# Edge loop of a message-passing layer: TensorE's signals moved from its matmuls to drain instructions

## The chip, the cores and the metric

One core of one Trainium2 chip runs the whole program. The metric is the device time of one execution in microseconds; the kernel before was run three times, and its median is compared with that of the kernel after.

## What is computed

A block of two layers works on 1,250 nodes with 512 features each. The first is a message-passing layer over 41,250 edges, the second a mixture of eight experts with top-k choice of nodes. Only the edge part of the first is touched by the change. Per edge, with `f_ij` 20 radial features, `r_ij` a vector and `rcut_ij` a weight:

```python
h = shifted_softplus(f_ij @ Wf1 + bf1)                 # first layer
W = (h @ Wf2 + bf2) * rcut_ij[:, None]                 # second layer
m_s = s2 * W[:, :2 * F]                                # s2, v2: products of source node rows and the direction
m_v = (v2.reshape(e, 2 * F, 3) * W[:, 2 * F:4 * F, None]).reshape(e, 6 * F)
agg = jax.ops.segment_sum(x_ij, idx_i, num_segments=n) # sum over edges that share a target node
```

Two linear maps, a softplus and the experts follow.

## The kernel before, in words

The edges are sorted by target node into tiles of 128, 344 tiles in all. Each tile belongs to one bucket of at most 64 target nodes, so that the segment sum of a tile is a product of a one-hot matrix (128 edges by 64 nodes) with the edges' messages. Four tiles make a quad (`QUAD`), and there are 86 quads (`QUADS`). Three quads (`RING`) are one body of a loop that runs 27 times after a first body is written out; the last two quads are written out behind the loop (`step` with `left` 1 and 0). All matmuls of the loop are in float32; one matmul of the code shows as two records of a weight load and two of a matmul, two passes.

Per quad `q` the engines do this, each in the order of its own program:

- POOL gathers edge records (`recs`, L529) and rows of the source nodes (`gath`, L540), one DMA for each per tile. The gather of a source row waits for `s_done` of an earlier tile (ring of six, `GRING`).
- PE: the four matmuls of the first layer for quad `q + 1` (`first_layer`, L1032, they signal `m1_done`), then four second layers for quad `q` (`second_layer`, L1041, one PSUM bank each, they signal `w_ready`), then four sums (`sum_tile`), and between sum 1 and sum 2 a transpose of the records of quad `q + 2` (`transpose_records`, L1026, it signals `t_done`). A sum has two halves that use different columns of the array: `plain` (L1053, two matmuls) and `scaled` (L1060, three matmuls); it signals `s_done` twice, by `plain(1)` and by `scaled(2)`. A sum waits for `prod_ready`, for the one-hots (`ohy_ready`) and for the flush of the bank that it writes (`flushed`, two banks in turn, `SRING`).
- DVE: `products` of the four tiles (L886, L888, L890; they wait for the rows gathered and for `w_ready`, and signal `prod_ready`), then for each tile `flush` (L901, adds the sum to the bucket's block in SBUF; it waits for both increments of `s_done` of its tile and signals `flushed`) and the one-hot of the next quad's tile (L877, `oneh`), and behind the second tile `hidden` (L868, `h_ready`). Products of quad `q + 1` stand behind flush 3 and one-hot 3 of quad `q`.
- ACT: the softplus of quad `q + 1` (L651, waits for `m1_done`; L655, L661), the seeds of the second layers' banks with the bias (L673, `seeded`), the scaled one-hots (L666) and the copy of the transposed records (L646, waits for `t_done`).
- SP prefetches weights for later stages, some of them paced by `prod_ready`.

Of the kernel before, what the change touches and what calls it, by code (L numbers as in the profile page):

```python
# [15 lines left out]
P = 128  # L16
# [106 lines left out]
def build(nc, x, src, rec_in, w_s, w_v, wf1, bf1, wf2, bf2, w1s, w1v, w2s, w2v,  # L123
          wg, wu, bu, wd, bd, out):
    ctx = ExitStack()
    with ctx:
# [3 lines left out]
        def sem(name):  # L130
            return ctx.enter_context(nc.semaphore(name))
# [37 lines left out]
        recs = sb("recs", [P, RING, QUAD, REC])  # L169
        rec_t = sb("rec_t", [P, RING, P])  # L170
# [14 lines left out]
        ident = sb("ident", [P, P])  # L185
# [10 lines left out]
        wf1_sb = sb("wf1_sb", [P, QUAD, FDIM])  # L196
# [33 lines left out]
        ps_h = PS[:, 4, :]  # L230
        ps_t = PS[:, 7, 0:P]
# [53 lines left out]
        t_done = sem("t_done")  # L285
        rec_t_ready = sem("rec_t_ready")
        m1_done = sem("m1_done")
# [4 lines left out]
        w_ready = sem("w_ready")  # L292
# [3 lines left out]
        s_done = sem("s_done")  # L296
# [99 lines left out]
        with nc.Block() as block:  # L396
# [531 lines left out]
            def _(pe):  # L928
# [4 lines left out]
                                 skip_group_check=True).then_inc(s_base, 1)  # L933

                for b in range(BUCKETS):
                    pe.wait_ge(s_pick, b + 1)
                    last = nc.tensor.matmul(ps_place, ident[:, :], by_bucket(scan)[:, b, :], start=b == 0,
                                            stop=b == BUCKETS - 1)
# [25 lines left out]
                def add_column(n):  # L964
# [3 lines left out]
                    if by_scalar(n):  # L968
# [8 lines left out]
                                 start=True, stop=True).then_inc(s_cps, 1)  # L977
# [16 lines left out]
                for k in range(TCOLS):  # L994
                    last = nc.tensor.transpose(PS[0:1, 4, k * P:(k + 1) * P], tile_f[:, 1, k:k + 1], ident[:, :])
# [27 lines left out]
                def transpose_records(q, r, body):  # L1023
                    pe.wait_ge(recs_in[r], 16 * QUAD * body + 16 * QUAD)
                    hold(pe, rec_t_ready, q + 1, pe_passed)
                    nc.tensor.transpose(ps_t, recs[:, r].rearrange("p k c -> p (k c)"), ident[:, :]).then_inc(t_done, 1)  # L1026

                def first_layer(q, r):

                    pe.wait_ge(rec_t_ready, q + 2)  # L1030
                    for k in range(QUAD):
                        last = nc.tensor.matmul(ps_h[:, k * P:(k + 1) * P], wf1_sb[:, k, :], rec_t[:, r, :],  # L1032
                                                start=k == 0, stop=k == QUAD - 1, skip_group_check=True)
                    last.then_inc(m1_done, 1)

                def second_layer(q, r, k, slot):

                    pe.wait_ge(h_ready, q + 1)
                    pe.wait_ge(seeded, QUAD * q + k + 1)  # L1040
                    nc.tensor.matmul(ps_w[slot], h_t[:, r, k * P:(k + 1) * P],  # L1041
                                     wf2_sb[:, :, :].rearrange("p k f -> p (k f)"),
                                     start=False, stop=True, skip_group_check=True).then_inc(w_ready, 1)

                def sum_tile(t, slot, bank, first=False):

                    pe.wait_ge(prod_ready, t + 1)
                    pe.wait_ge(ohy_ready, t + 1)
                    if not first:
                        pe.wait_ge(flushed, t - SRING + 1)  # L1050

                    def plain(half):
                        return nc.tensor.matmul(  # L1053
                            PS[0:WIDE, bank, half * 2 * FDIM:(half + 1) * 2 * FDIM], oneh[:, slot, 0, :],
                            prod[:, slot, 2 * half:2 * half + 2, :].rearrange("p k f -> p (k f)"),
                            start=half == 0, stop=half == 1, skip_group_check=True)

                    def scaled(i):
                        to = PS[WIDE:P, bank, :].rearrange("p (k f) -> p k f", k=4)[:, i:4:3 - i, :]
                        return nc.tensor.matmul(to, oneh[:, slot, 1 + i, :],  # L1060
                                                prod[:, slot, P_Q:P_B + i + 1:1 + i, :],
                                                start=i == 0, stop=i == 2, skip_group_check=True)

                    scaled(0)
                    plain(0)
                    scaled(1)
                    plain(1).then_inc(s_done, 1)
                    scaled(2).then_inc(s_done, 1)

                def step(q, r, body, left=2):  # L1070
                    if left >= 1:
                        pe.wait_ge(h_ready, q + 1)
                        first_layer(q + 1, (r + 1) % RING)
                    for k in range(QUAD):
                        second_layer(q, r, k, k)
                    for k in range(QUAD):
                        sum_tile(QUAD * q + k, k, k % SRING, first=isinstance(q, int) and q == 0 and k < SRING)
                        if k == 1 and left >= 2:
                            transpose_records(q + 2, (r + 2) % RING, body + (r + 2) // RING)

                transpose_records(0, 0, 0)
                first_layer(0, 0)
                transpose_records(1, 1, 0)
                for r in range(RING):
                    step(r, r, 0)
                with pe.Fori(1, BODIES) as i:
# [554 lines left out]
```

## Time and profile before

| | us |
|---|---|
| median of three runs | 1791.46 |
| lowest, highest | 1783.09, 1799.77 |
| profiled execution | 1775.62 |
| its span, first to last instruction | 1773.9 |

| engine | busy us | share of the span |
|---|---|---|
| PE, matmuls | 1373.2 | 77% |
| PE, weight loads | 811.7 | 46% |
| DVE | 1077.8 | 61% |
| ACT | 839.3 | 47% |
| POOL | 746.5 | 42% |

The mean granted clock of TensorE over the span was 0.960 of full speed. Times of day in the text are microseconds from the start of the span of this execution. Waits are idle stretches of an engine with the event that ended them, as far as the profile can tell; "remote" and "issue" stand where it names no instruction. PE is the matmul side of TensorE, PEld its weight loads, and a q behind an engine's name is its sequencer.

### The profile page before, as it was taken

The page shows a single profiled execution, that of the slowest core. Times are in us where ns is not written, and L with a number is a line of the kernel's source. Part 1 is how long each engine was busy: PE and PEld are TensorE (multiplying, and loading weights), DVE is VectorE, ACT ScalarE, POOL GpSimd, SP SyncE. Part 2 cuts the span into 40 slices and gives each one's busy share as a digit, 9 for nine tenths or more (in the row PEclk, how much of TensorE's full clock was granted, in tenths as well). Part 3 has the DMA queues.
Part 4 walks back from the last instruction along what each step waited for, and adds up shares of the span by engine and source line. Part 5 has one row for each costly group of instructions (what it writes and reads, how often), then busy time and mean ns, then how long its engine had stood idle before and what let it go on. Part 6 is the DMA issues. An engine that isn't in the chain of part 4 may idle for free. (4 is left out here: it accounts for less than half of the span.)

```text
span 1773.9 us, 27789 instructions
## 1 busy us (share of the span) xinstructions
PE 1373.2 (77%) x7164; PEld 811.7 (46%) x7164; DVE 1077.8 (61%) x2846; ACT 839.3 (47%) x2239; POOL 746.5 (42%) x798
## 2 busy tenths in 40 slices
PE   0787587777877877787777778777778629999997
PEld 0552344444444444444444444444445525665554
DVE  6899466766676667667676766776677752111110
ACT  3689455555555555555555555555555501111111
POOL 3200455555555555555555555555553011112211
PEclk9989799999999999999999999999999859999999
DMA  5142123333323333333333233332333432645531
GB/s 204 46 170 83 47 76 82 93 87 95 98 82 89 86 94 95 92 99 94 87 109 85 82 82 87 82 82 82 82 82 67 141 115 75 184 141 156 171 77 23
DMA packets 65893, 173.20 MB, mean 98 GB/s; under 512 B 14027, under 2 KB 22619, under 8 KB 65213
## 3 DMA queue, kind: packets, MB, share of 16 engines
q0 software_dynamic: 43648, 106.09, 23.2%
q1 hardware_dynamic: 22196, 66.57, 10.5%
q8 instruction: 17, 0.28, 0.1%
q14 instruction: 32, 0.26, 0.1%
HBM read 149.28 MB, written 18.08 MB: 94 GB/s over the span
## 5 line engine op out<-in xcount | busy, mean ns | idle before, releaser
L1060 PE MATMUL PS<-prod,oneh 128*64 128x256 f32 x2064 | 495.6, 391 | 255.4 <-DVE prod L890 149.8
L540 POOL DMA_INDIRECT gath<-table_d,recs x344 | 325.0, 945 | 406.2 <-PE PS L1060 164.3
L666 ACT ACTIVATE oneh<-oneh,recs 128x64 f32<-128x64 f32 x1032 | 283.5, 338 | 422.4 <-DVE oneh L877 387.3
L1060 PEld LDWEIGHTS PS<-prod,oneh 128*64 128x64 f32 x2064 | 274.6, 140 | 446.6 <-issue 226.7
L901 DVE TENSOR_TENSOR region_s<-region_s,PS 128x512 f32 x344 | 235.2, 684 | 327.9 <-remote 318.7
L529 POOL DMA_INDIRECT recs<-rec_d,inv_i x344 | 324.9, 944 | 209.7 <-issue 181.4
L1053 PE MATMUL PS<-prod,oneh 128*64 128x256 f32 x1376 | 364.8, 400 | 0.0
L1041 PE MATMUL PS<-wf_sb,h_t 128*128 128x512 f32 x688 | 310.5, 594 | 0.0
L673 ACT COPY PS<-c_rep 128x512 f32<-128x512 f32 x340 | 198.9, 585 | 92.2 <-DVE prod L890 89.5
L888 DVE TENSOR_TENSOR prod<-PS,gath 128x384 f32<-128x384 f32 x344 | 187.4, 545 | 0.0
L890 DVE TENSOR_TENSOR prod<-PS,gath 128x384 f32<-128x384 f32 x344 | 187.2, 544 | 0.0
L1041 PEld LDWEIGHTS PS<-wf_sb,h_t 128*128 128x128 f32 x688 | 124.6, 191 | 124.3 <-issue 124.3
L886 DVE TENSOR_TENSOR prod<-PS,gath 128x256 f32<-128x256 f32 x344 | 141.9, 413 | 38.8 <-remote 28.7
L1053 PEld LDWEIGHTS PS<-prod,oneh 128*64 128x64 f32 x1376 | 155.5, 138 | 0.7 <-issue 0.2
L877 DVE TENSOR_SCALAR oneh<-iota_f,recs 128x64 f32<-128x64 f32 x344 | 115.0, 335 | 6.7 <-DMA recs<-rec_d,inv_i 6.7
L1454 ACT ACTIVATE region_s<-PS,bu_col 128x312 f32<-128x312 f32 x64 | 33.3, 520 | 165.3 <-PE PS L1569 165.3
L1032 PE MATMUL PS<-rec_t,wf_sb 128*128 128x128 f32 x688 | 101.4, 291 | 0.8 <-ACT rec_t L646 0.8
L1032 PEld LDWEIGHTS PS<-rec_t,wf_sb 128*128 128x128 f32 x688 | 84.9, 194 | 34.0 <-issue 33.4
L1512 DVE TENSOR_TENSOR gath<-PS,region_x 128x512 f32<-128x512 f32 (+2 forms) x24 | 14.5, 602 | 139.1 <-PE PS L1584 115.7
L1419 POOL DMA_INDIRECT out<-gath,idx_add x24 | 39.7, 1654 | 128.9 <-ACT gath L1461 127.1
L970 PE MATMUL PS<-region_r 128*128 128x344 bf16 x323 | 72.4, 319 | 27.0 <-DVE region_r L819 10.9
L1409 POOL DMA_INDIRECT region_x<-xn_d,idx_e x24 | 24.1, 1003 | 162.6 <-DVE idx_e L1486 156.8
(272 smaller groups left out, 1537.9 us busy)
## 6 DMA issues: line engine op xcount, KB each, us to landing
region_r<-wu SPq DMA_DIRECT2D x16, 512.0 KB
region_r<-wd SPq DMA_DIRECT2D x16, 512.0 KB
region_u<-wu SPq DMA_DIRECT2D x16, 512.0 KB, 4.3
region_u<-wd SPq DMA_DIRECT2D x16, 512.0 KB, 5.4
recs<-rec_d,inv_i POOLq DMA_INDIRECT x344
gath<-table_d,recs POOLq DMA_INDIRECT x344
region_u<-rec_in SPq DMA_DIRECT2D x1, 5168.0 KB, 17.3
rec_d<-region_u SPq DMA_DIRECT2D x1, 5168.0 KB
```

What stands on the lines that cost most here:

```text
L529: nc.gpsimd.indirect_dma_start(out=recs[:, q % RING, k, :], out_offset=None, in_=rec_d, in_offset=bass.IndirectOffsetOnAxis(ap=inv_i[:, t: ...
L540: nc.gpsimd.indirect_dma_start(out=gath[:, t % GRING, :], out_offset=None, in_=table_d, in_offset=bass.IndirectOffsetOnAxis(ap=recs[:, q % ...
L666: last = nc.scalar.activation(oneh[:, slot, 1 + i, :], oneh[:, slot, 0, :], ACT.Copy, scale=recs[:, r, k, R_VEC + i:R_VEC + i + 1])
L673: nc.scalar.copy(ps_w[slot], c_rep[:, :]).then_inc(seeded, 1)
L886: nc.vector.tensor_tensor(prod[:, slot, P_A:P_Q + 1:P_Q - P_A, :], w[:, W_A:W_Q + 1, :], s.unsqueeze(1).to_broadcast([P, 2, FDIM]), ALU.mult)
L888: nc.vector.tensor_tensor(prod[:, slot, P_D:P_D + 3, :], w[:, W_D:W_D + 1, :].to_broadcast([P, 3, FDIM]), v, ALU.mult)
L890: nc.vector.tensor_tensor(prod[:, slot, P_B:P_B + 3, :], w[:, W_B:W_B + 1, :].to_broadcast([P, 3, FDIM]), v, ALU.mult).then_inc(prod_ready, 1)
L901: nc.vector.tensor_tensor(block, block, PS[:, bank, :], ALU.add).then_inc(flushed, 1)
L1032: last = nc.tensor.matmul(ps_h[:, k * P:(k + 1) * P], wf1_sb[:, k, :], rec_t[:, r, :], start=k == 0, stop=k == QUAD - 1, skip_group_check= ...
L1041: nc.tensor.matmul(ps_w[slot], h_t[:, r, k * P:(k + 1) * P], wf2_sb[:, :, :].rearrange("p k f -> p (k f)"), start=False, stop=True, skip_g ...
L1053: return nc.tensor.matmul(PS[0:WIDE, bank, half * 2 * FDIM:(half + 1) * 2 * FDIM], oneh[:, slot, 0, :], prod[:, slot, 2 * half:2 * half + ...
L1060: return nc.tensor.matmul(to, oneh[:, slot, 1 + i, :], prod[:, slot, P_Q:P_B + i + 1:1 + i, :], start=i == 0, stop=i == 2, skip_group_chec ...
```

## The change

In the edge loop, no matmul increments a semaphore any more. Behind the second layer of tile 1 PE drains and adds 2 to `w_ready`, then adds 1 to `m1_done` for the first layer that ran ahead of the second layers; behind the second layer of tile 3 it drains and adds 2 to `w_ready`. Behind each sum it drains and adds 2 to `s_done`; behind that of sum 2 it adds 1 to `t_done` for the transpose that stands between sum 1 and sum 2. The start of the loop gets two drains for the first transposes and the first layer. Nothing is changed on the other engines, in what is computed, or in the order of PE's matmuls.

```diff
--- before.py
+++ after.py
@@ -1023,15 +1023,14 @@
                 def transpose_records(q, r, body):
                     pe.wait_ge(recs_in[r], 16 * QUAD * body + 16 * QUAD)
                     hold(pe, rec_t_ready, q + 1, pe_passed)
-                    nc.tensor.transpose(ps_t, recs[:, r].rearrange("p k c -> p (k c)"), ident[:, :]).then_inc(t_done, 1)
+                    nc.tensor.transpose(ps_t, recs[:, r].rearrange("p k c -> p (k c)"), ident[:, :])
 
                 def first_layer(q, r):
 
                     pe.wait_ge(rec_t_ready, q + 2)
                     for k in range(QUAD):
-                        last = nc.tensor.matmul(ps_h[:, k * P:(k + 1) * P], wf1_sb[:, k, :], rec_t[:, r, :],
+                        nc.tensor.matmul(ps_h[:, k * P:(k + 1) * P], wf1_sb[:, k, :], rec_t[:, r, :],
                                                 start=k == 0, stop=k == QUAD - 1, skip_group_check=True)
-                    last.then_inc(m1_done, 1)
 
                 def second_layer(q, r, k, slot):
 
@@ -1040,7 +1039,7 @@
                     pe.wait_ge(seeded, QUAD * q + k + 1)
                     nc.tensor.matmul(ps_w[slot], h_t[:, r, k * P:(k + 1) * P],
                                      wf2_sb[:, :, :].rearrange("p k f -> p (k f)"),
-                                     start=False, stop=True, skip_group_check=True).then_inc(w_ready, 1)
+                                     start=False, stop=True, skip_group_check=True)
 
                 def sum_tile(t, slot, bank, first=False):
 
@@ -1064,8 +1063,8 @@
                     scaled(0)
                     plain(0)
                     scaled(1)
-                    plain(1).then_inc(s_done, 1)
-                    scaled(2).then_inc(s_done, 1)
+                    plain(1)
+                    scaled(2)
 
                 def step(q, r, body, left=2):
                     if left >= 1:
@@ -1073,14 +1072,25 @@
                         first_layer(q + 1, (r + 1) % RING)
                     for k in range(QUAD):
                         second_layer(q, r, k, k)
+                        if k == 1:
+                            pe.drain().then_inc(w_ready, 2)
+                            if left >= 1:
+                                pe.sem_inc(m1_done, 1)
+                    pe.drain().then_inc(w_ready, 2)
                     for k in range(QUAD):
                         sum_tile(QUAD * q + k, k, k % SRING, first=isinstance(q, int) and q == 0 and k < SRING)
+                        pe.drain().then_inc(s_done, 2)
+                        if k == 2 and left >= 2:
+                            pe.sem_inc(t_done, 1)
                         if k == 1 and left >= 2:
                             transpose_records(q + 2, (r + 2) % RING, body + (r + 2) // RING)
 
                 transpose_records(0, 0, 0)
+                pe.drain().then_inc(t_done, 1)
                 first_layer(0, 0)
                 transpose_records(1, 1, 0)
+                pe.drain().then_inc(m1_done, 1)
+                pe.sem_inc(t_done, 1)
                 for r in range(RING):
                     step(r, r, 0)
                 with pe.Fori(1, BODIES) as i:
```

## Rows read from the trace of the kernel before

**Rows 1.** Waits of the edge loop: total us, times, longest.

```profile
DVE region_s L901 <- remote: 318.7, 82, 4.8
```

**Rows 2.** Edge loop: window, us; busy PE, PEld, DVE, ACT, POOL.

```profile
206.00:1361.00 1155.00, 898.63 (x4843) 518.36 (x4843) 793.97 (x1790) 621.65 (x1702) 637.36 (x676) 0.98 0.32 88
```

**Rows 3.** L886: min/median/max ns, first and last start us.

```profile
L886 DVE TENSOR_TENSOR prod<-PS,gath x344: 406/411/425, 207.7 to 1363.1; 128x256 f32<-128x256 f32 x172
```

**Rows 4.** Timeline of DVE, one quad: start, length, operation [idle before].

```profile
799.88 0.42 DVE L886 TENSOR_TENSOR prod<-PS,gath 128x256 f32<-128x256 f32 x1
...
801.14 0.41 DVE L886 TENSOR_TENSOR prod<-PS,gath 128x256 f32<-128x256 f32 x1
...
804.92 0.67 DVE L901 TENSOR_TENSOR region_s<-region_s,PS 128x512 f32 x1
...
807.36 0.69 DVE L901 TENSOR_TENSOR region_s<-region_s,PS 128x512 f32 x1
...
812.30 0.69 DVE L901 TENSOR_TENSOR region_s<-region_s,PS 128x512 f32 x1 [3.95 <-remote]
...
813.13 0.42 DVE L886 TENSOR_TENSOR prod<-PS,gath 128x256 f32<-128x256 f32 x1
```

**Rows 5.** Timeline of PE and PEld, the same quad.

```profile
801.35 0.42 PE L1060 MATMUL PS<-prod,oneh 128*64 128x256 f32 x1 [1.57 <-DVE prod L890]
...
802.26 0.59 PE L1060 MATMUL PS<-prod,oneh 128*64 128x256 f32 x2
...
805.71 0.13 PEld L1060 LDWEIGHTS PS<-prod,oneh 128*64 128x64 f32 x1 [1.31 <-DVE prod L890]
...
807.49 1.03 PE L1060 MATMUL PS<-prod,oneh 128*64 128x256 f32 x4
...
808.44 0.97 PEld L1032 LDWEIGHTS PS<-rec_t,wf_sb 128*128 128x128 f32 x8 [0.38 <-issue]
...
809.33 0.30 PEld L1041 LDWEIGHTS PS<-wf_sb,h_t 128*128 128x128 f32 x2
809.44 3.60 PE L1041 MATMUL PS<-wf_sb,h_t 128*128 128x512 f32 x8
...
811.16 0.19 PEld L1041 LDWEIGHTS PS<-wf_sb,h_t 128*128 128x128 f32 x1 [0.24 <-issue]
811.59 0.19 PEld L1041 LDWEIGHTS PS<-wf_sb,h_t 128*128 128x128 f32 x1 [0.24 <-issue]
```

**Rows 6.** Timeline of POOL, the same quad.

```profile
812.95 0.94 POOL L540 DMA_INDIRECT gath<-table_d,recs  x1 [2.12 <-remote]
```

**Rows 7.** Timeline of PE and DVE, the two quads behind the loop.

```profile
1338.78 0.42 DVE L886 TENSOR_TENSOR prod<-PS,gath 128x256 f32<-128x256 f32 x1
...
1346.39 1.03 PE L1060 MATMUL PS<-prod,oneh 128*64 128x256 f32 x4
...
1347.55 0.69 DVE L901 TENSOR_TENSOR region_s<-region_s,PS 128x512 f32 x1 [0.38 <-PE PS L1060]
...
1349.48 0.42 DVE L886 TENSOR_TENSOR prod<-PS,gath 128x256 f32<-128x256 f32 x1 [1.01 <-PE PS L1041]
...
1359.29 0.42 DVE L886 TENSOR_TENSOR prod<-PS,gath 128x256 f32<-128x256 f32 x1
```

**Rows 8.** Timeline of DVE, one of the longer quads.

```profile
718.98 0.42 DVE L886 TENSOR_TENSOR prod<-PS,gath 128x256 f32<-128x256 f32 x1 [3.29 <-remote]
```

**Rows 9.** PE's drain at the block's end, and the last sum.

```profile
L396 PEldq DRAIN  x1: 1888/1888/1888, 1366.1 to 1366.1; - x1
...
1366.91 1.03 PE L1060 MATMUL PS<-prod,oneh 128*64 128x256 f32 x4
```

**Rows 10.** PE's sequencer by line: ns, first and last start.

```profile
L1040 PEldq EVENT_SEMAPHORE  x4: 51/51/51, 1346.3 to 1346.7; - x4
...
L1040 PEldq ALU_OP  x3: 32/32/32, 807.7 to 807.9; - x3
...
L1086 PEldq COMPARE_BRANCH  x27: 76/208/233, 289.9 to 1345.7; - x27
```

## The prediction

> **What bounds the kernel now.** The page comes first: PE is busy for 77% of the span, DVE for 61%, nothing for 100%, so the answer lies in waits inside a repeated pattern. The table by stretch says where the time is: the edge loop, from 206 to 1361 us, is 1155 of 1773.9 us, and only there is anything changed [rows 2]. Its unit is a quad of four tiles. The first product of quad 0 starts at 207.7 us [rows 3] and that of quad 85 at 1359.29 [rows 7]: 1151.6 us for 85 periods, 13.55 on average. The waits, grouped, show the stretch's largest wait without a producer: DVE stands 318.7 us, 82 times, 3.9 us each, ahead of a flush (L901), released by "remote" [rows 1]. That is once a quad.
>
> The timeline of one quad shows where. A period runs from 799.88 to 813.13, 13.25 us. DVE multiplies four tiles, starts flush 0 at 804.92 and flush 2 at 807.36, and then flush 3 starts only at 812.30, after 3.95 us idle [rows 4]. A flush waits for s_done alone (and for DVE's own last flush). But the sum that it waits for ended on PE at 807.49 + 1.03 = 808.52 [rows 5]. DVE is 3.8 us late for a signal whose work is done. POOL's gather behind the same sum also starts only at 812.95 after a "remote" wait [rows 6]: two engines miss the same event, so it is the increment that is late, not a reader. PE's second layers start at 809.44 and run for 3.60 us [rows 5], to 813.04, so the flush is let go inside that run. The next product needs the flush, the one-hot and w_ready; it starts at 813.13, although the second layer of its own tile ended near 809.44 + 0.43 + 0.59 = 810.46.
>
> The two quads behind the loop, whose waits have constants, are a control. There flush 3 starts at 1347.55, released by PE itself after 0.38 us, 0.13 behind the sum's end at 1346.39 + 1.03, and the periods are 1349.48 - 1338.78 = 10.70 and 1359.29 - 1349.48 = 9.81 us [rows 7]. So late increments may cost up to 2.5 us a quad.
>
> **What a drain costs.** The block's own drain on PE starts at 1366.1 and takes 1.888 us, to about 1367.99, where the last sum ended at 1366.91 + 1.03 = 1367.94 [rows 9]: it ends with the engine's work, 0.05 us behind. The rest of the price is what the sequencer did ahead of time before and does afterwards now. Where its waits follow each other, four waits start in 1346.3 to 1346.7, 0.13 apart, and three register operations in 807.7 to 807.9, 0.10 apart [rows 10]. I take 0.12 for each sequencer instruction behind a drain.
>
> **The change, step by step, as one turn of PE** from the drain behind the first pair of second layers (D1) to the next. Per quad six drains and two sequencer increments replace fourteen increments of matmuls. Their removal I cost at nothing by itself: eight passes with four increments among them end in 3.60 us, which is seven steps of 0.43 and the last one's 0.59 with nothing left over [rows 5].
> - Second pair: 3.60 less four passes of 0.43 is 1.88, and 0.11 from weight load to matmul (809.33 to 809.44) that is no longer hidden: 1.99.
> - Four sums: 801.35 to 802.26 + 0.59 is 1.50 for one that starts on an idle PE [rows 5]; 6.00 in all.
> - The transpose: 0.10, by the same load gap.
> - First layers: 808.44 to 809.44, 1.00; then the first pair, 1.88.
> - Six drains at 0.05: 0.30. Eleven sequencer instructions (increment and wait behind D1; two waits before sum 0; one before sum 1; two for the transposes and one before sum 2; t_done and a wait before sum 3; one before the first layer) at 0.12: 1.32. The branch, 0.208 and a register operation of 0.05, every third quad, was run ahead and now is not: 0.09 [rows 10].
>
> Sum: 1.99 + 6.00 + 0.10 + 1.00 + 1.88 + 0.30 + 1.32 + 0.09 = 12.68 us, against 13.25. PE becomes the ring that closes on itself. The others fit inside it. DVE starts its product about 0.13 after D1, reaches the end of flush 0 5.71 later (799.88 to 804.92 + 0.67) and PE could start sum 2 0.12 behind it (805.59 to 805.71) [rows 4, 5]: 5.96. PE arrives there at 0.24 + 1.99 + 0.05 + 0.24 + 1.55 + 0.12 + 1.55 + 0.36 + 0.10 = 6.20, later. Products take 1.26 each (799.88 to 801.14), so those of tiles 0 and 1 end some 1.4 and 2.7 behind D1, both before their sums (2.3 and 4.2). m1_done comes behind two second layers instead of behind the first layer, and so comes about when product 0 can start. ACT's next step behind the softplus that it feeds is a seed that waits for product 0, so a place at the product's start costs nothing; it would cost up to the pair's 1.88 us if ACT were the bound. t_done moves behind sum 2. On ACT the record copy waits for it, and the scaled one-hots of tiles 1 to 3 queue behind that copy; the copy is wanted by the first layer behind sum 3, some 1.8 us later (1.50, a drain and waits), the one-hots by sums of the next quad, so it costs nothing while sum 3 stands between. w_ready of tiles 0 and 2 waits for its pair: 0.86 us each, the first inside the ring above, the second hidden behind DVE's products 0 and 1.
>
> Bounds of the unknown price. If the waits fold away behind weight loads, the flush sets the start of sum 2: 5.96 + 1.55 + 0.12 + 1.55 + 0.10 + 0.09 + 1.00 + 1.88 + 0.05 = 12.30. If each drain costs 0.15 more than taken, 13.58. I take 12.7, nearest to the rows of the sequencer.
>
> Over the loop: 83 periods of (13.25 - 12.7) give 45.7 us. The 85 periods hold 1151.6 - 83 x 13.25 - 20.5 = 31 us more than the regular ones; part of it is the start, part are quads like the one in which, behind a late flush 3, the product itself waits 3.29 us more for "remote" [rows 8]. Signals from drains should end these: I take 15 of the 31, with 0 and 22 as bounds. The two last quads had prompt signals and lose: about 12.6 - 10.7 and 11.6 - 9.8, 3.7 us. Net 45.7 + 15 - 3.7 = 57 us. The profiled execution took 1775.62 us (span 1773.9), so 1718.6 there; the median shown is 1791.46, 15.8 above it, and 57 off the median is 1734.
>
> One rule speaks against this change. The Trainium skill, "PSUM — Partial Sum Buffer", section "Engine vs sequencer instructions", says to attach the increment to the matmul, since it fires at completion, and to put it on a drain only where a barrier is wanted, as a drain waits until the engine is idle. On drains this trace agrees (0.05 us); on matmuls it agrees in the last two quads and disagrees in the loop, 3.8 us. By the rule of the Trainium skill alone the change would add and give nothing.
>
> **The rivals.**
> - Cheap refill, the flush bounds: T = 12.30. 83 x 0.95 + 20 - 3 = 96, so 1695. For it: loads start 0.12 behind a signal, with sequencer work in that. Against: branch and register waits stand bare. 0.20.
> - Dear refill (the other side): the gain and the drains cancel where T is 13.25 + 11.3 / 83 = 13.39, that is 0.12 us more for each of six drains. Around that point, with 0.05 to 0.15 more each, it is 1758 to 1807, no change, 0.14; at 0.2 more, T = 13.88, 83 x 0.63 - 11 = 41 slower, 1832, 0.10. For it: nothing in this trace shows PE starting directly behind a drain.
> - The signal isn't the cause, or drains' signals are held too: the flush stays tied to the end of the second layers, which start 9.56 behind the product now and 1.3 later with the waits and drains laid bare. T = 13.25 + 1.3 + 0.4 = 14.95, 83 x 1.7 = 141 slower, 1932. This is where the rule of the Trainium skill named above leads. Against: the control quads. 0.05.
> - As forecast: T 12.5 to 13.0, 1709 to 1763. 0.51.
>
> **How the numbers follow.** A measurement of this kernel can tell about 1%, so faster is below 1773.5. Faster: 0.51 + 0.20 and a little of the middle case, 0.72. Within 1%: what is left of that case, 0.13. Slower: 0.10 and 0.05, 0.15. The range reaches from the cheap refill to the middle of the break-even case, 1692 to 1792.
>
> **What would show it.** The quad's period should be 12.7; flush 3 should follow sum 3 within 0.2 us and its "remote" wait be gone; PE should hardly wait for products or flushes; the gap from one sum's last matmul to the next load should be 0.2 to 0.3. The prediction is wrong if that gap is over 0.4, or if DVE still idles before flush 3.

## The result, and the profile after

The kernel after took 2217.14 us (median of four, 2214.69 to 2219.33), the kernel before beside it 1790.82 (1783.09 to 1799.77): a ratio of 1.238, 95% interval 1.232 to 1.244. The forecast was 1734, with a range up to 1792. It failed on the wrong side and by 483 us.

The page of the kernel after, busy time by engine and TensorE's granted clock in 40 slices of the span:

```profile
PE 1590.0 (72%) x7164; PEld 867.1 (39%) x7164; DVE 1082.9 (49%) x2846; ACT 856.3 (39%) x2239; POOL 747.8 (34%) x798
...
PEclk9897888888888888888888888888888896799999
```

The digit of the granted clock is now 8 tenths through nearly the whole edge loop. The table by stretch over the whole loop, which now ends near 1805 (columns as in [rows 2], the last three being clock, DMA share and GB/s):

```profile
206.00:1805.00 1599.00, 1119.37 (x4862) 577.14 (x4861) 800.66 (x1794) 639.74 (x1707) 637.93 (x675) 0.86 0.23 64
```

So 1599 us where the kernel before took 1155 at 0.98 [rows 2]: the whole loss is in the loop. Outside it next to nothing moved: the first product comes 3 us later, and what follows the start of the last one takes some 410 us in both. L886 gives the mean quad, its first start being tile 0's and its last tile 343's:

```profile
L886 DVE TENSOR_TENSOR prod<-PS,gath x344: 410/411/427, 210.7 to 1805.2; 128x256 f32<-128x256 f32 x172
```

The last quad's first product starts 3.8 us ahead of its last, three times 1.26, so 85 quads take 1805.2 - 3.8 - 210.7 = 1590.7 us, 18.71 each (median 19.3), against 13.55 before and 12.88 in the forecast (1151.6 less 57, by 85). The waits of the loop, grouped (total, times, longest):

```profile
POOL gath L540 <- PEq L1082: 762.8, 162, 8.3
DVE region_s L901 <- PEq L1082: 398.1, 147, 5.1
ACT oneh L666 <- DVE oneh L877: 378.0, 104, 5.2
DVE prod L886 <- PEq L1076: 375.3, 86, 5.2
PEld PS L1032 <- issue: 361.3, 84, 5.3
PE PS L1032 <- issue: 323.6, 84, 4.8
ACT soft L651 <- PEq L1078: 295.2, 80, 4.5
```

The releaser "remote" of [rows 1] is gone in name: the late signal now is the drain's (L1082). What is new is the row of PE itself: it stands 323.6 us, 84 times, ahead of a first layer (L1032), where it stood for nothing before. One quad of the kernel after shows how; first PE, then its drain behind sum 3, then DVE and POOL:

```profile
1014.00 0.59 PE L1059 MATMUL PS<-prod,oneh 128*64 128x256 f32 x2
1018.74 1.96 PE L1032 MATMUL PS<-rec_t,wf_sb 128*128 128x128 f32 x8 [4.14 <-issue]
1020.49 2.78 PE L1040 MATMUL PS<-wf_sb,h_t 128*128 128x512 f32 x4
1023.64 1.98 PE L1040 MATMUL PS<-wf_sb,h_t 128*128 128x512 f32 x4 [0.36 <-issue]
```

```profile
L1082 PEldq DRAIN  x1: 5288/5288/5288, 1013.2 to 1013.2; - x1
```

```profile
1012.89 0.69 DVE L901 TENSOR_TENSOR region_s<-region_s,PS 128x512 f32 x1 [0.50 <-PEq L1082]
...
1018.58 0.69 DVE L901 TENSOR_TENSOR region_s<-region_s,PS 128x512 f32 x1 [4.78 <-PEq L1082]
```

```profile
1009.76 0.94 POOL L540 DMA_INDIRECT gath<-table_d,recs  x1 [8.19 <-PEq L1082]
1011.01 0.94 POOL L529 DMA_INDIRECT recs<-rec_d,inv_i  x1 [0.30 <-PEq L1082]
...
1016.02 0.94 POOL L529 DMA_INDIRECT recs<-rec_d,inv_i  x1 [0.30 <-issue]
1019.24 0.94 POOL L540 DMA_INDIRECT gath<-table_d,recs  x1 [2.28 <-PEq L1082]
```

The last matmul of sum 3 ends at 1014.00 + 0.59 = 1014.59. The drain behind it was issued at 1013.16, lasts 5.288 us and ends at 1018.45: 3.85 us after the engine's work, with PE empty. Among the 344 drains at L1082, 76 end more than 0.5 us behind their last matmul, 291 us in sum, all of them behind sum 3; the others end 0.02 us behind. In the same stretch POOL issues six gathers, one every 1.25 us, and the trace has the last landing of the sixth (a record gather) at 1018.44, 0.01 us ahead of the drain's end. Then PE works slowly. Granted clock is the third number from the end:

```profile
1013.00:1014.60 1.60, 1.48 (x10) 0.84 (x10) 0.81 (x2) 1.60 (x7) 1.16 (x2) 1.00 0.32 77
1018.70:1020.70 2.00, 1.96 (x9) 1.97 (x10) 0.80 (x2) 0.82 (x3) 1.16 (x2) 0.55 0.00 0
1020.70:1022.40 1.70, 1.70 (x3) 0.67 (x3) 0.00 (x0) 0.00 (x0) 0.73 (x1) 0.53 0.61 158
1022.40:1024.00 1.60, 1.24 (x4) 0.34 (x3) 0.67 (x2) 0.52 (x1) 0.00 (x0) 1.00 0.06 6
```

Full clock (2.4 GHz) during sum 3, some half of it (1.2 GHz) in the 3.7 us behind the idle stretch, then full again. The Trainium skill, "TensorE: Matmul & The Clock Gate", part "The HAM clock gate", says the same: an idle engine is clocked at the lower level until activity releases it.

So two things stand against each other here that I had not put in the sum: a drain that ends late, and a clock that is low behind it (e7 tests whether the idle stretch is the reason). Neither needs, so far, that a signal was moved.

### The profile page after: what moved, and what is told of

The parts are those of the page before. It is cut to its first block and busy times, and to the rows that moved or that the text cites. A ratio compares the mean times of both kernels' runs of the same rounds, so it can differ in the third digit from the quotient of the medians.

```text
span 2214.7 us, 28477 instructions
## 1 busy us (share of the span) xinstructions
PE 1590.0 (72%) x7164; PEld 867.1 (39%) x7164; DVE 1082.9 (49%) x2846; ACT 856.3 (39%) x2239; POOL 747.8 (34%) x798
## 5 line engine op out<-in xcount | busy, mean ns | idle before, releaser
L540 POOL DMA_INDIRECT gath<-table_d,recs x344 | 325.4, 946 | 845.7 <-PEq L1082 762.8
L1059 PE MATMUL PS<-prod,oneh 128*64 128x256 f32 x2064 | 517.1, 387 | 84.5 <-issue 61.2
L1040 PE MATMUL PS<-wf_sb,h_t 128*128 128x512 f32 x688 | 439.7, 774 | 46.8 <-issue 46.8
L666 ACT ACTIVATE oneh<-oneh,recs 128x64 f32<-128x64 f32 x1032 | 276.0, 338 | 399.3 <-DVE oneh L877 378.0
L1032 PE MATMUL PS<-rec_t,wf_sb 128*128 128x128 f32 x688 | 167.5, 420 | 326.9 <-issue 323.6
L1059 PEld LDWEIGHTS PS<-prod,oneh 128*64 128x64 f32 x2064 | 255.8, 137 | 329.3 <-issue 176.3
L1052 PE MATMUL PS<-prod,oneh 128*64 128x256 f32 x1376 | 373.5, 394 | 0.0
L886 DVE TENSOR_TENSOR prod<-PS,gath 128x256 f32<-128x256 f32 x344 | 142.7, 415 | 382.0 <-PEq L1076 375.3
L1032 PEld LDWEIGHTS PS<-rec_t,wf_sb 128*128 128x128 f32 x688 | 143.6, 309 | 365.2 <-issue 361.3
L1040 PEld LDWEIGHTS PS<-wf_sb,h_t 128*128 128x128 f32 x688 | 157.0, 253 | 272.2 <-issue 272.2
L651 ACT ACTIVATE soft<-PS,b1col 128x512 f32<-128x512 f32 x86 | 59.1, 687 | 318.6 <-PEq L1078 295.2
L1052 PEld LDWEIGHTS PS<-prod,oneh 128*64 128x64 f32 x1376 | 161.0, 137 | 0.0
L877 DVE TENSOR_SCALAR oneh<-iota_f,recs 128x64 f32<-128x64 f32 x344 | 120.2, 350 | 7.0 <-DMA recs<-rec_d,inv_i 7.0
L816 DVE TENSOR_SCALAR region_r<-iota_h,region_x 128x344 bf16<-128x344 f16 x323 | 91.8, 325 | 0.1
```

The source lines that it names most:

```text
L540: nc.gpsimd.indirect_dma_start(out=gath[:, t % GRING, :], out_offset=None, in_=table_d, in_offset=bass.IndirectOffsetOnAxis(ap=recs[:, q % ...
L666: last = nc.scalar.activation(oneh[:, slot, 1 + i, :], oneh[:, slot, 0, :], ACT.Copy, scale=recs[:, r, k, R_VEC + i:R_VEC + i + 1])
L886: nc.vector.tensor_tensor(prod[:, slot, P_A:P_Q + 1:P_Q - P_A, :], w[:, W_A:W_Q + 1, :], s.unsqueeze(1).to_broadcast([P, 2, FDIM]), ALU.mult)
L1040: nc.tensor.matmul(ps_w[slot], h_t[:, r, k * P:(k + 1) * P], wf2_sb[:, :, :].rearrange("p k f -> p (k f)"), start=False, stop=True, skip_g ...
L1052: return nc.tensor.matmul(PS[0:WIDE, bank, half * 2 * FDIM:(half + 1) * 2 * FDIM], oneh[:, slot, 0, :], prod[:, slot, 2 * half:2 * half + ...
L1059: return nc.tensor.matmul(to, oneh[:, slot, 1 + i, :], prod[:, slot, P_Q:P_B + i + 1:1 + i, :], start=i == 0, stop=i == 2, skip_group_chec ...
```

## The experiments

The first group of runs asks whether the late completion comes from GpSimd's gathers, and which drains matter. Its kernel before took 1787.55 us.

**e1, the kernel before with nearly no record gathers.**

```
 def gather_record(t):
+    if q >= RING: return
     nc.gpsimd.indirect_dma_start(out=recs[...] ...)
 # and the waits on recs_in for the first landing only
```

> The kernel before, from the fourth quad on without the record gathers (L529): the records of the first three quads are used again, all waits on them ask for the first landing only; the output is not the reference's. POOL issues four indirect DMAs a quad instead of eight. Theory A (what PE finishes is reported late while POOL issues indirect DMAs back to back, until the last of the batch has landed): the late signal of sum 3 goes, the quad falls from 13.3 to about 10.7 us as in the two last quads, 83 x 2.6 = 215 us and some 15 of the longer quads: about 1560 us. Theory B (the late report comes of PE's own program, the turn from half-array sums to full-array matmuls): the quad stays at 13.3, 1780 to 1800 us.

1537.46 us, ratio 0.859 (0.854 to 0.864). DVE's "remote" wait ahead of the flush, 318.7 us [rows 1], has no row left in it; what DVE waits for is released by PE's own matmuls:

```profile
DVE prod L888 <- PE PS L1043: 78.7, 82, 2.1
...
DVE region_s L903 <- PE PS L1062: 33.0, 79, 1.6
```

POOL issues 332 gathers fewer and never six in a row: the four that are left of a quad go in two pairs, 1.30 us apart within a pair and 2.09 between them. That PE's signals were late in the kernel before is thus something that the gathers bring about. A cost of the gathers themselves goes too, so this run alone doesn't give the price of the late signals.

**e2, the same cut in the kernel after.**

> The changed kernel with the same gathers left out (records of the first three quads used again). Theory A: the drain behind sum 3 ends 0.02 us behind its last matmul instead of 3.85, PE doesn't go idle there and its clock stays at the upper level; the quad falls from 19.3 to the 12.7 us that the prediction worked out: 2217 - 83 x 6.6 - 10 = about 1660 us. Theory B: nothing changes, about 2217 us.

1731.11 us, ratio 0.967 (0.962 to 0.973). The drain behind each sum, in e2:

```profile
L1084 PEldq DRAIN  x344: 1293/1458/1570, 214.6 to 1322.5; - x172
```

No drain behind a sum lasts longer than 1.57 us, where the kernel after has up to 5.58. This kernel has the drains and all moved signals, and its median quad is 12.9 us, its mean 12.98, beside 12.68 and 12.88 in the forecast. The refill and the drains cost what was worked out. Against e1, where a quad takes 10.76, they cost 2.2 us a quad: with prompt signals on both sides the change is a loss of 194 us.

**e3, the kernel after with sum 3 signalling by its matmuls again.**

```
-                        pe.drain().then_inc(s_done, 2)
+                        if k < 3:
+                            pe.drain().then_inc(s_done, 2)
 # and in sum 3: plain(1).then_inc(s_done, 1); scaled(2).then_inc(s_done, 1)
```

> The changed kernel with one of six drains undone: sum 3 signals s_done by its own two matmuls again, the others by drains. If the loss sits in this drain (its 3.85 us of waiting on an idle PE, and the half clock of the nine matmuls behind it, some 2.6 us), the quad falls from 19.3 to 12.9 or, since the next drain then falls into the late stretch and waits for its end, to at most 13.5: 1690 to 1790 us. If each drain were dear by itself, it would fall by a sixth of the 6 us only: about 2130 us.

1831.08 us, ratio 1.023 (1.016 to 1.030), nearer to the first theory, yet 41 us above its range. PE no longer stands ahead of the first layers, but the drain behind the first pair of second layers is now the one that ends late, and DVE's old wait is back:

```profile
DVE region_s L901 <- remote: 346.5, 77, 4.9
...
PE PS L1040 <- issue: 129.3, 84, 5.6
```

77 times 4.5 us, and the flush starts 3.7 us behind its sum: s_done from a matmul is as late as from a drain. Whatever reports PE's work is late for some stretch of each quad; what differs is whether PE has something to do meanwhile. With a drain behind sum 3 it has nothing, with the increment on the matmul it goes on into the layers.

**e4, the kernel after with second and first layers signalling by their matmuls, the sums by drains.**

> The changed kernel with its two drains behind the second layers undone: second layers and first layer signal by their matmuls, the four sums by drains. If the loss sits in the drain behind sum 3, it stays: only the two drains and the bare waits behind them go, some 0.3 us each, and product 0 starts a matmul earlier, at the half clock up to 1.7 us; quad 18 to 19 us, 2110 to 2200 us. If the drains of the second layers carried the loss, it would come near the kernel before.

2090.58 us, ratio 1.168 (1.161 to 1.175), a little below the range that was expected. The idle time of PE ahead of a first layer is as in the kernel after (busy us, mean ns, then idle):

```profile
L1032 PE MATMUL PS<-rec_t,wf_sb 128*128 128x128 f32 x672 | 150.8, 394 | 314.9 <-issue 314.9
```

Of the 426 us lost, 303 come with the sums' drains alone.

The second group asks which gathers do it, and prices the clock and the drains by themselves; the kernel before took 1796.78 us.

**e5, the kernel before with nearly no source-row gathers (L540).**

> The kernel before, with L540 issued only for the first six tiles (later tiles take the old rows, so the output differs); the record gathers L529 all stay. It is the mirror image of the run without most record gathers (1537 us). If what holds PE's completions back is a batch of GpSimd's gathers without a gap, of either kind, then half the gathers leave no hold: 1500 to 1600 us, and the three w_ready and two s_done of a quad come one by one. If it is the record gathers themselves, whatever stands beside them, the hold stays: 1720 to 1800 us.

1533.51 us, ratio 0.854 (0.850 to 0.858). DVE's wait ahead of a flush has no "remote" row left, the largest is 23.4 us. Either half of the gathers without the other leaves PE's signals prompt. Whether the kind or the number or the distance matters, e1 and e5 can't tell: both leave four a quad, in the same pairs.

**e6, the kernel before with full pauses.** Behind every gather:

```
+                    pause(nc.gpsimd.memset(idle[:, :], 0.0))   # 128x256 bf16, waited for
```

> The kernel before, and behind each of the 688 gathers in the edge loop GpSimd sets 128x256 bf16 of an idle tile to zero (some 0.35 us), which nothing reads. All gathers stay, but no two of them are issued 1.25 us apart. If a run of gathers without a gap holds PE's completions back, quads become shorter although GpSimd has more to do: eight times some 1.6 us make 12.8 a quad at the most, 1600 to 1750 us. If the number of gathers decides, or their landing, the hold stays and the longer batch makes it longer: 1790 to 1900 us.

2061.51 us, ratio 1.148 (1.142 to 1.153): far above both ranges. The pause was dearer than I had put it: a memset of 0.33 us and 0.81 us of waiting for it make 2.09 us a gather, 16.7 a quad.

```profile
1001.31 0.95 POOL L544 DMA_INDIRECT gath<-table_d,recs  x1 [0.81 <-PE PS L1065]
1002.26 0.33 POOL L548 MEMSET idle<- 128x256 bf16 x1
1003.39 0.95 POOL L532 DMA_INDIRECT recs<-rec_d,inv_i  x1 [0.81 <-ACT oneh L671]
```

POOL is the bound here. No "remote" wait of DVE is left, those ahead of a flush go by PE's matmuls (468.6 us over the loop), which is in line with the theory, but as an estimate of the gain the run is useless; e9 repeats it with a cheaper pause.

**e7, the kernel after with the idle stretch filled.** Ahead of the drain behind sum 3:

```
+                        if k == 3 and left >= 1:
+                            pe.wait_ge(h_ready, q + 2)
+                            for n in range(4):
+                                nc.tensor.matmul(ps_h, h_t[:, r, n * P:(n + 1) * P], wf2_sb[...],
+                                                 start=True, stop=True, skip_group_check=True)
                         pe.drain().then_inc(s_done, 2)
```

> The kernel after, with four more matmuls of 128x512 behind sum 3 ahead of its drain, which write ps_h where the next first layer begins anew, so that nothing reads them: 8 passes, some 3.5 us a quad of additional work for PE, in the stretch in which it stood idle behind sum 3. If the hold ends at a moment that GpSimd's batch sets, and the idle stretch is what lowered PE's clock, the drain ends no later than before, and the first and second layers behind it run at full clock: 19.3 less some 2 a quad, 2000 to 2100 us, with more work than the kernel after. If the hold begins only when PE is done, the 3.5 us come on top: 2450 to 2550 us. If it ends where it did but the clock falls anyway: 2200 to 2250 us.

2074.75 us, ratio 1.155 (1.150 to 1.161): 142 us faster than the kernel after, with 3.7 us more of matmuls in each quad. The first fence is a quad of e7 on PE, the second the whole loop by stretch:

```profile
1022.24 3.70 PE L1085 MATMUL PS<-wf_sb,h_t 128*128 128x512 f32 x8
...
1026.98 1.15 PE L1032 MATMUL PS<-rec_t,wf_sb 128*128 128x128 f32 x8 [1.05 <-issue]
1027.97 1.88 PE L1040 MATMUL PS<-wf_sb,h_t 128*128 128x512 f32 x4
```

```profile
206.00:1660.00 1454.00, 1253.40 (x5531) 603.23 (x5532) 797.52 (x1789) 640.49 (x1711) 637.72 (x676) 1.00 0.26 70
```

The clock is 1.00 in place of 0.86. First layers and first pair take 1.15 and 1.88 us in place of 1.96 and 2.78. The drain behind the filled stretch, issued at 1020.93, ends at 1026.32 in the trace, 5.39 us later, where the one without the filling took 5.29: its end is set by something outside PE. Both halves of the expectation hold, and the clock by itself is worth these 142 us, 1.7 a quad. The same drain, as long, stands in both kernels, so it is the idle stretch that lowers the clock and not the drain.

**e8, the kernel before with bare drains.** No signal moved:

```
                         sum_tile(QUAD * q + k, ...)
+                        pe.drain()
```

> The kernel before with a drain behind each of the four sums, which signals nothing; all signals stay at the matmuls, as they were. If a drain waits until PE's completions are let go, PE cannot begin the next first layer behind sum 3 before that: 13.2 a quad becomes 18 to 20, 2130 to 2250 us, as slow as the kernel after with no signal moved at all. If a drain ends with the last matmul and only its signal is late, the drains cost their refills alone, four times some 0.5 us a quad and little of it on the path: 1790 to 1980 us.

2092.97 us, ratio 1.165 (1.160 to 1.171). This is below the first theory's range by 37 us and above the second's by 113; the rows decide for the first. PE stands 250.2 us ahead of the first layers, the loop's clock is 0.89, and 153 of the drains end more than 0.5 us late:

```profile
L1032 PE MATMUL PS<-rec_t,wf_sb 128*128 128x128 f32 x672 | 151.5, 396 | 250.2 <-issue 250.2
```

Four drains that signal nothing cost as much (ratio 1.165) as four that carry s_done (e4, 1.168, the intervals overlap). Moving the signals of the sums was neither gain nor loss; what costs is that PE may not go on.

The third group varies the distance between gathers; the kernel before took 1790.74 us. The pause is now waited for only ahead of the next one, and so costs POOL no more than its own time:

```
+                    pause.wait()
+                    pause.add(nc.gpsimd.memset(idle[:, :], 0.0))
```

**e9, the kernel before, pause of 128x256.**

> The kernel before with the same write of zeros to 128x256 bf16 of an idle tile behind each gather of the edge loop, but GpSimd waits for it only ahead of the next such write, so that it costs its 0.33 us and no more: a gather every 1.6 us or so where the kernel before has 1.25 and the run with full pauses 2.1. Eight of them make 12.8 a quad. If any gap between gathers of more than 0.3 us ends the hold, GpSimd becomes the bound at 12.8: 1700 to 1770 us. If what counts is how many gathers are under way when PE's work ends, 1.6 is still too close, and the hold is there with a longer batch: 1800 to 1950 us.

1736.33 us, ratio 0.969 (0.964 to 0.975): faster than both kernels, with 688 instructions more, and in the first range, though not for its whole reason. A gather comes every 1.45 us. DVE's wait ahead of a flush falls from 318.7 to 181.0 us, so the late signals are shorter, not gone; flush 3 starts 2.4 us behind its sum in 81 quads, where it is 3.7 in 82 quads of the kernel before:

```profile
DVE region_s L908 <- remote: 181.0, 76, 3.4
```

**e10, the kernel before, pause of 128x32.**

> The same with 128x32 bf16, a pause as short as this instruction can be (below 0.1 us, so that a gather comes every 1.35 us): where GpSimd's instruction between two gathers is enough, whatever it takes, there is no hold and GpSimd has 10.8 a quad to do: 1560 to 1680 us, faster than both kernels. If the hold is one of distance in time, nothing changes: 1770 to 1850 us.

1790.64 us, ratio 1.000 (0.998 to 1.002). The memset takes 0.14 us and 0.17 is left as a gap, in all the same 0.3 us as between two gathers without it, so that the distance stays 1.25:

```profile
1001.80 0.95 POOL L545 DMA_INDIRECT gath<-table_d,recs  x1 [0.17 <-issue]
1002.74 0.15 POOL L550 MEMSET idle<- 128x32 bf16 x1
1003.06 0.95 POOL L532 DMA_INDIRECT recs<-rec_d,inv_i  x1 [0.17 <-issue]
```

That makes it a clean control: an instruction between two gathers does nothing, the distance in time does.

**e11, the pause of e9 behind record gathers only.**

> The same pause of 0.33 us, but only behind the record gathers L529, so that source and record gathers go in pairs 1.25 apart and the pairs stand some 2.85 apart in sum: 11.4 a quad for GpSimd. If a hold needs a row of three or more gathers without a gap, it is gone: 1600 to 1700 us. If not, 1770 to 1880 us.

1783.05 us, ratio 0.995 (0.992 to 0.998), the "remote" wait still 314.2 us. Pairs 1.25 us apart, one every 2.7 us, hold the signals as fully as the row without a pause: six gathers 1.25 us apart are not needed.

**e12, the kernel after with the pause of e9.**

> The kernel after with the 0.33 us pause behind each gather. If the hold is gone, what stays is the forecast's own quad of 12.7 for PE beside 12.8 for GpSimd: 1740 to 1850 us, against 2217 without the pause. If the hold stays: 2150 to 2350 us.

1913.03 us, ratio 1.068 (1.062 to 1.074): between the two ranges, a miss for both. 304 us are won, but 104 of the drains behind sums still end over 0.5 us late, by 1.3 us on average, up to

```profile
L1089 PEldq DRAIN  x344: 1320/1478/4058, 214.7 to 1504.7; - x172
```

4.06 us long. So at 1.45 us the effect is halved in both kernels. What was open here was whether a larger distance would end it, and whether it is the row or the number of gathers that counts.

The last group ran on a chip where the kernel before took 1772.61 us.

**e13, the kernel before, pause of 128x384 (0.43 us, a gather every 1.55).**

> The kernel before with a pause of 128x384 bf16 (some 0.45 us) behind each gather, so that one comes every 1.55 us or so against 1.45 with 128x256 and 1.25 without. If the hold shrinks with the distance alone and was all but gone at 1.45, GpSimd's eight times 1.55, 12.4 a quad, are now the bound: 1730 to 1790 us. If much of the hold was left at 1.45: 1640 to 1715 us.

1710.10 us, ratio 0.966 (0.963 to 0.968), the second of the two cases. The "remote" row is gone, in no quad does flush 3 start over 0.5 us behind its sum, and PE's next limit shows, the transpose that waits for records which POOL now fetches later:

```profile
PE PS L1033 <- DMA recs<-rec_d,inv_i: 149.2, 76, 5.5
DVE region_s L908 <- PE PS L1067: 146.4, 80, 6.6
```

This run also rules out two other causes. It issues all eight gathers of a quad, and with 12.72 us a quad in place of 13.55 it issues them at a higher mean rate than the kernel before; so neither their number nor their mean rate is what holds the signals.

**e14, the kernel before with one pause in each quad** (two waited memsets behind the quad's first record gather, meant to break the row beside sum 3).

> The kernel before with a single break of some 1.5 us a quad in GpSimd's row of six gathers, behind the record gather that is issued beside sum 3, and no other pause. If the hold of sum 3's signal ends when the last gather of an unbroken row has landed, the break lets it through about 2.2 us earlier, at the landing of the gather ahead of the break: s_done of sum 3 within 1.5 us of its end, and 1650 to 1760 us. If the hold depends on the number of gathers in a quad or on their mean rate, it stays: 1780 to 1850 us.

1751.94 us, ratio 0.988 (0.986 to 0.991), in the first range. DVE's "remote" wait ahead of a flush falls to 9.3 us, and flush 3 is late (over 0.5 us behind its sum) in 2 quads. But the row isn't shorter, it stands elsewhere: 66 rows of six and 13 of eight gathers 1.25 us apart are left, where the kernel before has 77 and 1. The late signals went with it. w_ready is late in part of the quads (DVE waits 145.8 us for L1047 ahead of a product), and flush 1, which in the kernel before waits once for a late sum, by 0.7 us, is late in 30 quads, by 3.9 us on average. The profile puts these waits down to PE's matmuls and not to "remote". One such quad, with a row of eight:

```profile
1014.05 0.95 POOL L546 DMA_INDIRECT gath<-table_d,recs  x1 [0.82 <-POOL idle L537]
...
1022.79 0.94 POOL L532 DMA_INDIRECT recs<-rec_d,inv_i  x1 [0.30 <-issue]
```

```profile
1018.90 1.03 PE L1066 MATMUL PS<-prod,oneh 128*64 128x256 f32 x4
```

```profile
1025.52 0.69 DVE L907 TENSOR_TENSOR region_s<-region_s,PS 128x512 f32 x1 [3.27 <-PE PS L1059]
```

Sum 1 ends at 1018.90 + 1.03 = 1019.93, and its flush starts 5.59 us later.

**e15, the kernel before with one wait made stricter.**

```
-  hold(pool, s_done, 2 * (t - GRING + 2), pool_passed)
+  hold(pool, s_done, 2 * (t - GRING + (3 if k == 3 else 2)), pool_passed)
```

> The kernel before with one wait made stricter and no instruction more: the source gather of the fourth tile of a quad waits for one sum more (sum 3 in place of sum 2), so that the row is broken by a wait for PE itself. By the theory that the row's last landing lets the signals go, sum 3's signal comes at the landing of the gather ahead of the wait, some 1.3 us behind its matmuls in place of 3.6, but the rest of the row now lies beside the second layers, whose w_ready it can hold: 1700 to 1800 us. If PE's signals are late by a fixed time behind idle PE, GpSimd waits for it too and the quad grows: 1820 to 1950 us.

1722.58 us, ratio 0.972 (0.970 to 0.974), in the first range. Not an instruction more, a gather that waits longer, and the kernel is 2.8% faster. Its waits of DVE:

```profile
DVE region_s L901 <- PE PS L1060: 109.7, 72, 3.0
DVE prod L886 <- PE PS L1041: 98.5, 59, 5.1
DVE region_s L901 <- remote: 54.1, 27, 3.1
```

The number of gathers and POOL's busy time are those of the kernel before. Part of the rows is broken (49 of six are left, 68 are of four now), and part of the lateness stays or moves: flush 3 is late in 40 quads by 1.65 us (82 by 3.7 before), flush 1 in 43 by 3.2. So e14 and e15 show that which signal is late goes by where the row stands; that the gathers' number and mean rate are not the cause is shown by e13.

**e16, the kernel after with the pause of e13** (kernel before beside it: 1772.29 us).

> The kernel after with the longer pause, a gather every 1.55 us, at which distance the kernel before showed PE's signals one by one. If the late signals and the clock that falls behind them are all that the forecast left out, this kernel, which computes everything, runs at the forecast's own quad of 12.7, or at GpSimd's 12.4: 1730 to 1810 us, level with the kernel before. If the drains have a further cost of their own, it stays near the 1913 us of the shorter pause: 1880 to 1950 us.

1744.63 us, ratio 0.985 (0.981 to 0.989). This is the kernel after, computing everything. The drains behind its sums last 2.26 us at most, no drain ends over 0.5 us late, its mean quad is 13.13 us, and its clock 0.99:

```profile
206.00:1336.00 1130.00, 950.16 (x4872) 482.47 (x4872) 822.69 (x1799) 646.37 (x1715) 938.11 (x1356) 0.99 0.33 91
```

With the same pauses on both sides the change loses (1744.63 here, 1710.10 in e13). What it wins against the plain kernel before is the pauses' doing.

Here the miss can be added up, kernel after less e16, from two rows of each (busy us, mean ns, idle before). The kernel after:

```profile
L1040 PE MATMUL PS<-wf_sb,h_t 128*128 128x512 f32 x688 | 439.7, 774 | 46.8 <-issue 46.8
L1032 PE MATMUL PS<-rec_t,wf_sb 128*128 128x128 f32 x680 | 165.4, 420 | 326.5 <-issue 323.6 <-DVE h_t L868 2.9
```

and e16:

```profile
L1047 PE MATMUL PS<-wf_sb,h_t 128*128 128x512 f32 x688 | 333.8, 608 | 31.6 <-issue 31.6
L1039 PE MATMUL PS<-rec_t,wf_sb 128*128 128x128 f32 x680 | 98.9, 289 | 37.2 <-issue 34.3 <-DVE h_t L875 2.9
```

Idle ahead of the first layer: 326.5 - 37.2 = 289 us, the late drains. Busy in layers: (439.7 - 333.8) + (165.4 - 98.9) = 172 us, the clock. Together 461, of the 470 between the two profiled spans (2214.7 and 1744.3).

## Why the prediction was wrong, point by point

- **The step that failed is the price of a drain.** I took "it ends with the engine's work, 0.05 us behind" from one drain at the block's end [rows 9], which stands behind the loop, where no record gather is under way. Inside the loop the drain behind sum 3 ends some 3.8 us behind, in 76 of 86 quads, and PE stands idle 289 us for it. In the evidence that I had, [rows 1, 4 and 6] showed that PE's increments are late in the loop. I read this as a fault of the matmul's increment, which a drain would not share, and gave the case that it does a chance of 0.05. e3 (DVE waits 4.5 us, 77 times, for s_done from matmuls) and e8 (drains without signals late) show that the report of PE's completed work is late, whoever asks for it. The control quads [rows 7] that spoke against this rival are quads with one record gather (at 1339.85) between them and no row of more than two: they differed from the loop in the true cause, and I took them for a test of the waits.
- **What a drain does with a late report was not followed.** In the kernel before the late report costs only those who wait for it, and PE goes on into the layers. A drain makes PE itself wait. The rival of 1932 us had the late signal tied to the second layers' end and 1.3 us more a quad; in fact PE's whole idle stretch lies on the ring: 12.9 + 3.4 (289 by 84) + 2.0 (172 by 86) = 18.3, against 18.71 measured.
- **The clock had no term.** The sum took all durations at full clock, right while PE is busy at 0.98 [rows 2]. An idle stretch of 4.14 us brings the layers behind it to half clock: 142 us by e7, 172 by the rows. Even had the late drain been in the sum, this would have been missing.
- **The refill was right.** 12.68 us a quad, put together from rows of sequencer instructions, is 12.9 in the median quad of e2, and 13.06 in that of e16. The part that was too small is the branch: in e2 the quads with one take 13.31 and the others 12.90 and 12.80, so 0.4 to 0.5 more and not 0.26. Removed increments of sums cost nothing, as taken: the ratios of e4 and e8 differ by 0.003.
- **The 15 us from longer quads** was not tested by itself; in e2 such quads are gone (the longest takes 13.39 us), in the kernel after they can't be told from the late drains.
- **The tail** came as forecast in direction, dearer in size: 13.12 and 11.38 us in the last two quads of the kernel after, beside 12.6 and 11.6 forecast and 10.70 and 9.81 before [rows 7]; 4.0 us in sum, 3.7 forecast.
- **The signs I had named** did show it: "if DVE still idles before flush 3" (4.78 us in the quad above). The period is 19.3 and not 12.7; the gap ahead of a load, 0.23 to 0.38 us on PE, stays below the 0.4 that I had named.
- The Trainium skill's rule from the prediction ("PSUM — Partial Sum Buffer", section "Engine vs sequencer instructions": increments on the matmul, a drain only as a barrier) led to the right side. By e2 against e1 its reason, that a drain waits for an empty engine, is worth 194 us. What it states besides, that the increment fires at completion, the loop contradicts: in e3 the flush starts 3.7 us behind matmuls that signal by themselves. And the drain, which by that section waits for an idle engine, ends 3.85 us behind the last matmul here, with the engine idle.

## What to carry to other kernels

When a signal comes late though its work is done, find out first who else is active in that stretch and not where it is active in the control; then ask whether the replacement goes through the same report. An experiment that takes half of the suspected neighbour away (e1) would have pointed to it in one run. A drain turns lateness that only readers paid for into idle time of the engine, and on TensorE that time is paid twice, since the clock falls. And a faster engine can be the fault: here GpSimd, with time to spare, issued its gathers as closely as it could, and holding it back (a stricter wait, e15, or a pause of 0.43 us, e13) gave 2.8% and 3.4% that no change to the signals could.

## What the runs showed of the hardware

- Completions of TensorE, of matmuls and of drains, can be reported some 4 us late while GpSimd issues indirect DMAs in a row, one every 1.25 us (0.94 of it busy); pairs 1.25 us apart, one every 2.7 us, do the same (e11). At a distance of 1.45 us the lateness is about half (181.0 for 318.7 us of DVE's wait), at 1.55 none is left, though the gathers' number is the same and their mean rate higher (e13). In the kernel before the reports then come in a burst, 0.04 us apart.
- In the kernel after, 85 of the loop's drains end over 0.5 us late (76 behind sums, 9 behind second layers). For 76 of the 85 that end lies within 0.04 us of a recorded landing of a gather, nearly always of the record gather that ends the row; 0.3 us earlier or 1 us later there is hardly such a landing for any. Where the row was shifted or broken (e14, e15), other signals were late. That the landing lets them go is what these places in time suggest. By which path GpSimd's gathers keep TensorE's reports back stays open, and so does whether one kind of gather would do it at the full number and distance (e1 and e5 left half of them); it wasn't tried with plain DMAs or with a full queue of another engine.
- TensorE's granted clock was 0.55 and 0.53 in the 3.7 us behind an idle stretch of 4.14 us, and 1.00 where useless matmuls filled it (e7).
- A drain behind work of its engine costs TensorE 0.02 us itself when the report is prompt; with its refill, six of them cost 2.2 us a quad (e2 against e1).
